# Transformer layer on one core: token parts held against both weight parts in one product of 512 columns, and half of the key transposes moved from TensorE to VectorE and DMAs

## Time and profile before

| what | value |
|---|---|
| median of 3 runs | 1308.89 us (1308.15 to 1309.69) |
| the profiled execution's own time | 1308.92 us |
| its span (first to last instruction) | 1307.1 us |
| granted TensorE clock | 0.999 of 2.4 GHz |
| PE busy | 1287.2 us, 98% |
| DVE busy | 1144.3 us, 88% |
| POOL busy | 830.8 us, 64% |
| ACT busy | 707.8 us, 54% |
| DMA engines busy (mean of 16) | about 24% |

### The profile page before, as it was taken

The page is one execution under the profiler, slowest core; times in us unless marked ns, Lnnn a source line. Parts: engine busy times, 40 slices in busy tenths (PEclk is TensorE's granted clock), DMA queues, the critical chain, the costliest instruction groups (busy, mean ns, idle before and its releaser), DMA issues.

```text
span 1307.1 us, 55818 instructions
## 1 busy us (share of the span) xinstructions
PE 1287.2 (98%) x24160; PEld 1116.5 (85%) x24160; DVE 1144.3 (88%) x2686; ACT 707.8 (54%) x1487; POOL 830.8 (64%) x673
## 2 busy tenths in 40 slices
PE   5999999999999999999999999999999999999998
PEld 4888888888888888888888888888888888888887
DVE  7988898888898888988888988889888889888885
ACT  5645655455654456554555544565545555445552
POOL 2676665765666756657656667566576566675554
PEclk9999999999999999999999999999999999999999
DMA  5012212222222222222222222221222222222211
GB/s 185 14 56 73 78 50 51 80 78 78 65 61 56 79 78 79 51 51 81 78 79 64 67 51 78 78 78 51 51 80 78 79 64 67 51 78 63 61 35 34
DMA packets 175860, 88.54 MB, mean 68 GB/s; under 512 B 135552, under 2 KB 171264, under 8 KB 171520
## 3 DMA queue, kind: packets, MB, share of 16 engines
q1 hardware_dynamic: 174912, 83.97, 22.6%
q10 hardware_dynamic: 704, 1.01, 0.2%
HBM read 53.18 MB, written 17.04 MB: 54 GB/s over the span
## 4 chain that ended last, share of the span: by engine, by line
PE 95%; DVE 3%; POOL 1%; issue 1%; ACT 0%; DMA 0%; DVEq 0%; POOLq 0%
PE ring L343 51%; PE scores L343 17%; PE ring L466 7%; PE ring L482 6%; PE scores L415 5%; PE state_sum L429 4%; PE ring L488 2%; PE scores L397 2%; DVE sm L895 1%; POOL xn L731 0%; DMA x_t<-in_L_attn_x_dram 0%; PE scores L352 0%; POOL rstd L722 0%; DVE stats L819 0%; POOL x_t L748 0%
## 5 line engine op out<-in xcount | busy, mean ns | idle before, releaser
L757 POOL TENSOR_TENSOR hid<-hid,cwb 128x512 f32<-128x512 f32 x128 | 166.4, 1300 | 181.8 <-DVE hid L924 181.0
L916 DVE SCALAR_TENSOR_TENSOR cT<-xT,conv_ws,cT 128x512 f32<-128x512 f32 x192 | 275.1, 1471 | 0.0
L745 POOL TENSOR_TENSOR x_t<-x_t,same 128x1024 f32<-128x1024 f32 x32 | 76.9, 2404 | 254.9 <-ACT same L618 254.9
L639 ACT ACTIVATE sg<-ring 128x512 f32<-128x512 f32 x128 | 76.6, 599 | 268.5 <-PE ring L343 268.5
L343 PE MATMUL ring<-xl,wgu_h 128*128 128x512 f32 x512 | 213.1, 416 | 0.0
L761 POOL TENSOR_TENSOR hl<-hid,hh 128x512 fp32r<-128x512 f32 x128 | 208.8, 1632 | 0.0
L343 PE MATMUL ring<-xh,wgu_l 128*128 128x512 f32 x512 | 201.0, 393 | 0.3 <-issue 0.3
L343 PE MATMUL ring<-xh,wgu_h 128*128 128x512 f32 x512 | 200.5, 392 | 0.0
L569 ACT ACTIVATE yh<-yT 128x256 fp32r<-128x256 f32 x128 | 53.5, 418 | 246.7 <-DVE yT L933 246.7
L902 DVE TENSOR_TENSOR state_bd<-state_sum,tables_s 128x256 f32<-128x256 f32 x248 | 104.0, 419 | 93.8 <-PE state_sum L429 90.6
L895 DVE TENSOR_TENSOR sm<-scores,causal_s 128x512 f32<-128x512 f32 x256 | 157.7, 675 | 6.0 <-PE scores L415 5.0
(11 more groups left out here) (134 smaller groups left out, 3453.4 us busy)
## 6 DMA issues: line engine op xcount, KB each, us to landing
cwb<-cw_rows SPq DMA_DIRECT2D x32, 1024.0 KB, 4.6
x_t<-in_L_attn_x_dram SPq DMA_DIRECT2D x32, 512.0 KB, 4.2
out_dram<-x_t SPq DMA_DIRECT2D x31, 512.0 KB, 2.9
xT<-qks_tok SPq DMA_DIRECT2D x896, 16.0 KB, 1.8
cw_rows<-cwt SPq DMA_DIRECT2D x128, 2.0 KB, 1.4
sm<-in_L_attn_wqkv_dram ACTq DMA_DIRECT2D x2, 384.0 KB, 5.0
sm<-in_L_ffn_Wg_dram SPq DMA_DIRECT2D x2, 256.0 KB, 3.8
sm<-in_L_ffn_Wu_dram SPq DMA_DIRECT2D x2, 256.0 KB, 4.6
```

The costliest lines, as they stand in the source:

```text
L639: act.activation(sg[:, :], GB[t % 2], ACT.Silu).then_inc(s_sg, 1)
L745: pool.tensor_tensor(xb, xb, same[:, :, :], ALU.add).then_inc(s_base1, 1)
L757: pool.tensor_tensor(hid[:, e, :], hid[:, e, :], cwb[:, e, :], ALU.mult).then_inc(s_hid, 1)
L916: ins = dve.scalar_tensor_tensor(out=cT[:, c, :], in0=xT[:, third(s, j, 0), c, LEAD - HALO + n:LEAD - HALO + n + BT], scalar=conv_ws[:, c, ...
```

## The change

- **Output stage.** The weights `wd` and `wo_s` hold low and high part side by side (512 columns). `both_parts` multiplies the high token part by both at once (512 columns, a whole bank), then the low token part by the high weights (256 columns, right half of the bank). The bank holds two sums, and VectorE adds both to x, one after the other.
- **Keys.** For all batches but the first, TensorE transposes the keys of tiles 0 and 1 alone (4 transposes in place of 8). `turn_keys` on VectorE transposes those of tiles 2 and 3 in blocks of 32 x 32 into `kb` (the room of `hid[:, 2]`), and `place_keys` moves the blocks to `ktok` with 16 DMAs of 16 KB from SyncE. VectorE waits for them before it writes `hid[:, 2]`, TensorE before the state sum of tile 2.
- **Taps.** Where the next batch is turned by blocks, ScalarE makes the products of taps 1 to 3 (`tap_terms`, six activations of 128x512 from SBUF into the PSUM banks `SB[0:2]`), and VectorE only adds them (`add_terms`). TensorE waits for the third before it writes the keys' banks.
- **DMAs of the turned input.** 24 of the 32 stay with SyncE, 8 go to ScalarE, one after each of its steps from `silu(1)` to `high_y(2)`.
- **Fill.** 12 waits after each of the first three experts of an output tile (8 in the first batches) and 6 (2) at the batch's start, in place of 38 at its start.
- **Statistics.** Batch 1 takes the statistics of batch 3 after tile 0 and of batch 4 where those of batch 3 stood; before, those of batch 4 came at the batch's very end.

```diff
-    FILL = 38
+    FILL = 12
-        wd_h, wd_l = sb("wd_h", [P, E, D], F32R), sb("wd_l", [P, E, D], F32R)
+        wd = sb("wd", [P, E, 2, D], F32R)
+        wd_l, wd_h = wd[:, :, 0, :], wd[:, :, 1, :]
...
+        kb = hid[:, 2, :].rearrange("p (a t g i) -> p a t g i", a=QUADS, t=2, g=C)
+        TB = SB[0:2]
...
SyncE, spread_cw:
+                if k:
+                    place_keys(s, j, k, range(1))
                 sp.wait_ge(cw_out, at(s, j, 16 * P // BLK, (k + 1) * 16 * P // BLK))
...
+            def place_keys(s, j, k, quarters):
+                sp.wait_ge(s_kturn, at(s, j, 1, k))
+                for a in quarters:
+                    for q in range(QUADS):
+                        sp.dma_start(ktok[a * BLK:(a + 1) * BLK, 2:4, :, q * BLK:(q + 1) * BLK],
+                                     kb[q * BLK:(q + 1) * BLK, a, :, :, :]).then_inc(ktok_in, 16)
SyncE, batch:
-                    place_turned(s, j, 2)
+                    place_turned(s, j, 2, 0, range(QUADS))
+                    place_turned(s, j, 2, 1, range(QUADS // 2))
                 if left:
                     spread_cw(s, j, 1)
+                    place_keys(s, j, 1, range(1, QUADS))
TensorE, heads:
+                if k and by_blocks(s, j, k):
+                    pe.wait_ge(s_conv, at(s, j, HALO, HALO))
...
-                    for t in range(T):
+                    for t in range(T // 2 if k else T):
TensorE, state_sum:
+                if n == T and s + j:
+                    pe.wait_ge(ktok_in, keys_at(s, j, k))
TensorE, batch:
+                def both_parts(dst, hi, lo, w, first=False, final=False):
+                    mm(dst[:, 0:2 * D], hi, w, start=first, stop=False, skip_group_check=True)
+                    return mm(dst[:, D:2 * D], lo, w[:, D:2 * D], start=False, stop=final, skip_group_check=True)
...
+                def fill(n):
+                    for _ in range(n if by_blocks(s, j, 1) else n - 4):
+                        pe.wait_ge(tables_in, 16)
...
                         ins = add_hidden(t, dst, e)
+                        if e < E - 1:
+                            fill(FILL)
...
-                if not last and by_blocks(s, j, 1):
-                    for _ in range(FILL):
-                        pe.wait_ge(tables_in, 16)
+                fill(FILL // 2)
ScalarE:
+            def place_turned(s, j, n):
+                if n == 0:
+                    act.wait_ge(s_turn, at(s, j, 1, 3 - BY_PE))
+                    act.wait_ge(s_halo, at(s, j, 1, 1))
+                a, q = QUADS // 2 + n // QUADS, n % QUADS
+                row = xT[q * BLK:(q + 1) * BLK, third(s, j, 2), 1, LEAD:LEAD + BT]
+                act.dma_start(row.rearrange("p (t a n) -> p t a n", t=T, a=QUADS)[:, :, a, :],
+                              xb_t[a * BLK:(a + 1) * BLK, 1, q, :, :]).then_inc(xT_in[1], 16)
...
+                def tap_terms(n):
+                    if n == 1:
+                        act.wait_ge(s_sm, at(s, j, U * ROWS, U * ROWS))
+                    else:
+                        act.wait_ge(s_conv, at(s, j, HALO, n - 1))
+                    for c in range(C):
+                        first = LEAD - HALO + n
+                        ins = act.activation(TB[c][:, :], xT[:, third(s, j, 0), c, first:first + BT], ACT.Copy,
+                                             scale=conv_ws[:, c, n:n + 1])
+                    ins.then_inc(s_tapped, 1)
order: silu(1) DMA high_hid(0) DMA tap_terms(1) DMA high_y(1) DMA silu(2) DMA high_hid(1) DMA tap_terms(2) DMA
       high_y(2) DMA silu(3) high_hid(2) tap_terms(3) high_y(3) high_hid(3)
VectorE:
+            def turn_keys(s, j, k):
+                for g in range(C):
+                    dve.wait_ge(s_kT, at(s, j, C, k * C + g + 1))
+                dve.wait_ge(s_hl, at(s, j, T, 3))
+                for t in range(2):
+                    ins = dve.transpose(kb[:, :, t, :, :].rearrange("p a g i -> p g a i"),
+                                        kT[:, :, (2 + t) * P:(3 + t) * P].rearrange("p g (a n) -> p g a n", n=BLK))
+                ins.then_inc(s_kturn, 1)
...
+                    for c in range(C):
+                        ins = dve.tensor_tensor(cT[:, c, :], TB[c][:, :], cT[:, c, :], ALU.add)
+                    ins.then_inc(s_conv, 1)
...
                     router(s, j, 1)
+                    turn_keys(s, j, 1)
                     key_sums(s, j, 1)
...
-                    dve.tensor_tensor(xb, done[:, 0:D], xb, ALU.add).then_inc(s_out, 1)
+                    own(dve.tensor_tensor(xb, done[:, 0:D], xb, ALU.add))
+                    dve.tensor_tensor(xb, done[:, D:2 * D], xb, ALU.add).then_inc(s_out, 1)
```

More of the change, by code:

```diff
@@ L300, in spread_cw, with place_turned @@
                              cw_rows.rearrange("r n -> (r n)").partition_broadcast(P)).then_inc(cw_in, 16)
-            def place_turned(s, j, k):
+            def place_turned(s, j, k, c, quarters):
                 sp.wait_ge(s_turn, at(s, j, 1, k + 1 - BY_PE))
                 sp.wait_ge(s_halo, at(s, j, 1, k - 1))
[L307 to L312, removed]
+                for a in quarters:
+                    for q in range(QUADS):
+                        row = xT[q * BLK:(q + 1) * BLK, third(s, j, k), c, LEAD:LEAD + BT]
+                        sp.dma_start(row.rearrange("p (t a n) -> p t a n", t=T, a=QUADS)[:, :, a, :],
+                                     xb_t[a * BLK:(a + 1) * BLK, c, q, :, :]).then_inc(xT_in[c], 16)
+            def place_keys(s, j, k, quarters):
+                sp.wait_ge(s_kturn, at(s, j, 1, k))
+                for a in quarters:
+                    for q in range(QUADS):
+                        sp.dma_start(ktok[a * BLK:(a + 1) * BLK, 2:4, :, q * BLK:(q + 1) * BLK],
+                                     kb[q * BLK:(q + 1) * BLK, a, :, :, :]).then_inc(ktok_in, 16)
             def batch(s, j, left):
@@ L493, in add_attention @@
                     pe.wait_ge(s_yl, at(s, j, T, t + 1))
[L494 to L495 removed]
+                    for c in range(C):
+                        both_parts(dst, yh[:, c, ts], yl[:, c, ts], wo_s[:, c, :, :].rearrange("p a n -> p (a n)"))
                 def add_hidden(t, dst, e, first=False):
                     ts = slice(t * P, (t + 1) * P)
[L499 to L500 removed]
+                    return both_parts(dst, hh[:, e, ts], hl[:, e, ts], wd[:, e, :, :].rearrange("p a n -> p (a n)"),
+                                      first=first, final=e == E - 1)
+                def fill(n):
+                    for _ in range(n if by_blocks(s, j, 1) else n - 4):
+                        pe.wait_ge(tables_in, 16)
                 def output(t):
@@ L669, in batch @@
                 high_y(0)
+                placing = left > 1 and by_blocks(s, j, 2)
                 silu(1)
+                if placing:
+                    place_turned(s, j, 0)
                 high_hid(0)
+                if placing:
+                    place_turned(s, j, 1)
+                if ahead:
+                    tap_terms(1)
+                if placing:
+                    place_turned(s, j, 2)
                 high_y(1)
+                if placing:
+                    place_turned(s, j, 3)
                 if not last and not ahead:
@@ L679, in batch @@
                 high_hid(1)
+                if placing:
+                    place_turned(s, j, 5)
+                if ahead:
+                    tap_terms(2)
+                if placing:
+                    place_turned(s, j, 6)
                 high_y(2)
+                if placing:
+                    place_turned(s, j, 7)
                 silu(3)
                 high_hid(2)
+                if ahead:
+                    tap_terms(3)
                 high_y(3)
@@ L774, in batch @@
                         low_x(s, j, 1, c)
+                if by_blocks(s, j, 3) and not by_blocks(s, j, 2):
+                    normalise(s, j, 2)
                 weigh(1)
@@ L789, in batch @@
                     base(s, j, 1)
-                if left > 1 and not by_blocks(s, j, 2):
+                if left > 1 and not by_blocks(s, j, 3):
                     normalise(s, j, 2)
@@ L908, in batch, with add_terms @@
                 last = left == 0
+                def add_terms(n):
+                    if n == 1:
+                        dve.wait_ge(s_tap0, at(s, j, 1, 1))
+                    else:
+                        dve.wait_ge(s_conv, at(s, j, HALO, n - 1))
+                    dve.wait_ge(s_tapped, (s * BPS + j - BY_PE + 1) * HALO + n)
+                    for c in range(C):
+                        ins = dve.tensor_tensor(cT[:, c, :], TB[c][:, :], cT[:, c, :], ALU.add)
+                    ins.then_inc(s_conv, 1)
                 def tap(n):
+                    if not last and by_blocks(s, j, 1):
+                        add_terms(n)
+                        return
                     if n == 1:
@@ L923, in gate_up @@
                     dve.wait_ge(s_up, at(s, j, T, t + 1))
+                    if t == 2 and s + j:
```

(10 more changed lines are left out.)

16 lines of the change are left out of this document (13 added, 3 removed).

## The result

In 20 runs of each kernel the time went from 1308.97 us (1308.15 to 1309.69) to 1311.32 us (1310.68 to 1312.26): ratio 1.0018, 95% interval 1.0012 to 1.0024. That is no gain but a loss of 2.35 us: the interval excludes 1, and its size is at the edge of the 0.2% that the prediction said can be told from no change. The forecast was 1294.5 us. The profiled execution has a span of 1309.0 us (1307.1 before) at the same granted clock, 0.999.

A forecast was written before the change was run, and what follows sets the result against it. PE was taken as the bound, its start-to-start distances making about 39.9 us a batch. 28 batches x (0.435 + 0.19 - 0.10) = 14.7, less 0.2, gave 14.5 us off 1308.92: 1294.5 us, range 1288 to 1308.

The forecast's parts named there:

- that of ScalarE: ScalarE's queue: six more activations and 8 DMA issues of 0.60 us fit into its gaps and cost nothing.
- Together about 0: First batches: 0.9 us new wait against 0.62 gained, three times, perhaps 0.5 for statistics, against a 1.2 us stall removed.
- output tiles: PE's output stage: 12 products instead of 18 save 0.05 us a tile, 0.19 us a batch; bounds 0 and 0.27.
- fill: Waits spread through PE's output stage: charged 0.1 us a batch, bounds 0 and 0.3.
- key transposes: PE's key stage: four of eight transposes go at 0.109 us each, saving 0.435 us a batch in 31 batches.
- VectorE's output chain: VectorE from router to last addition: starts 0.7 us earlier, grows by 0.72 and 1.78, just fits with 0.1 to 0.2 spare.
- last batch, in all: Program's end: the last batch adds one addition (0.44 us) and saves 0.2 us on PE.
- VectorE's chain: Rival at the batch's start: VectorE's longer output chain makes PE's numerators wait; 1299 to 1306 us, chance 0.15.
- The fill does not pace PE: Denies the rival that output-stage waits cost 0.3 us a batch instead of 0.1: 1300, up to 1304 us, chance 0.12.
- The slow rival: ScalarE's DMAs wait for SyncE's, up to 1.29 us per issue; silu late, PE stands about 0.85 us a batch; 1317, chance 0.12.
- It decides from about 1.05 us per issue: Threshold for ScalarE's and SyncE's queues blocking each other: below 1.05 us per DMA issue, silu(3) is on time.
- It does little: Rival on PE: columns stay the same and small stalls eat the transposes' 0.435 us; 1306 to 1311 us, chance 0.06.

The follow-up runs named there:

- Experiments 5: Kernel before with one change: 8 of the 32 DMAs of the turned input moved from SyncE to ScalarE; 1320.49 us, ratio 1.0086.
- experiment 6: Kernel after with the two ScalarE DMAs that fell into PE's bursts moved behind `high_y(2)` and `silu(3)`; 1304.0 us, ratio 0.9962 to the kernel before.
- 9: Kernel before with 8 DMAs on ScalarE and SyncE's 24 held until VectorE has written y of tile 2; run once, 1315.26 us beside 1309.08.
- experiment 7: Kernel after with batch 1's statistics in the order of the kernel before; 1309.8 us, ratio 1.0003 to the kernel before.
- 4: Kernel after with all eight key transposes on PE, no key DMAs, and 8 fill waits left out; 1320.17 us, ratio 1.0084 to the kernel before.
- 8: Kernel before with only the output stage changed: 512-column products, two additions, spread fill of 11 and 12; 1306.6 us, ratio 0.9981.
- experiment 3: Kernel after without any of the fill; 1333.45 us, ratio 1.0181 to the kernel before.
- experiments 1: Kernel after with all 32 DMAs of the turned input on SyncE again; 1366.3 us, ratio 1.0433 to the kernel before.
- experiments 2: Kernel after with all taps on VectorE again, the DMAs left on ScalarE; 1329.81 us, ratio 1.0156 to the kernel before.

## Why the prediction was wrong

**The step that failed** is that of ScalarE: six activations and 8 DMA issues, "Cost nothing". ScalarE's own queue is indeed on time, and its issues take about 0.60 us as taken (median 0.593). The step looked only for who waits for ScalarE and at the time the issue takes. It didn't ask what else runs while two queues issue. The runs show 0.19 + 0.27 = 0.46 us a batch on PE, 28 x 0.46 = 12.9 us in all. Experiments 5, 6 and 9 tie it to both queues being at it beside a burst of short products.

**"Together about 0"** for batches 0 to 2 was the second: +5.5 us, 3.1 of it by the statistics in batch 1 (experiment 7). I had counted these at half a microsecond. The rest of the chain, with taps still on VectorE there, I had at 0.9 us three times; PE waited 1.05, 1.56 and 1.07 us for the last addition at the start of batches 1, 2 and 3, which is 1.0 us more in sum.

**Where the 16.4 us between forecast and spans went** (14.5 forecast as gain, 1.9 measured as loss). In the 27 steady batches 0.52 - 0.16 = 0.36 is missing in each, 9.8 us: 0.46 for ScalarE's DMAs and 0.05 for the output tiles, less 0.10 for the fill, which cost nothing, and about 0.04 in stages that moved by less than 0.02 each. The first four batches make 6.0 (5.5, and 0.5 that was forecast as the gain of batch 3), the two ends of the program 0.5.

**Terms against forecast**, us a batch:

| term | forecast | measured | by |
|---|---|---|---|
| key transposes | -0.435 | -0.44 | stages, 4 |
| output tiles | -0.19 | -0.14 | stages, 8 |
| fill | +0.10 | 0 | 3 |
| VectorE's output chain | 0 | 0 | stages |
| ScalarE's DMAs | 0 | +0.46 | 5, 9 |
| first batches, in all | 0 | +5.5 | stages, 7 |
| last batch, in all | +0.24 | +0.64, and +0.13 ahead of batch 0 | stages, spans |

The output term was mis-sized in its pitch: it used that of products among their like, 0.228 and 0.118 us; in the mixed tile the experts' 512-column products lie 0.232 us before the next, and a tile saves 0.035 us, not 0.05. The Trainium skill (TensorE: Matmul & The Clock Gate, "Back-to-back issue gap") gives the 2.5 ns for an isolated warm product; the 0.06 us a batch worked out from it is an estimate, and the 0.14 measured decides.

**The rivals.** VectorE's chain did not become the bound: additions 0.42 to 0.45 us apart, as taken. The fill does not pace PE. The slow rival named the right two queues and the wrong mechanism: all 224 issues of ScalarE overlap one of SyncE, and yet 194 took 0.59 to 0.65 us, 29 up to 0.85 and one 1.65. So the lock that the Trainium skill describes (Perfetto Trace Analysis, "DMA Instruction — HWDGE (DVE, Sync)") is not visible in these durations. "It decides from about 1.05 us per issue" asked for a late silu, and the loss came without one. "It does little" comes closest to the measured time, with 1306 to 1311, and that is luck: no small stalls ate the transposes' 0.435 us, they were gained in full and given back in the bursts.

What stays open: why two queues slow the burst. The first half of a burst runs at its old pace: up to the 57th product the starts lie as before, to 1 ns in the mean of 18 bursts of tile 1 in the kernel after. The lag grows from about the 65th to 0.20 us at the 97th, and the last 16 add nothing. In experiment 6, where ScalarE's issue is over by then, the lag (0.08 us) falls into the same part. Nothing waits on a semaphore, so it looks like PE's supply of instructions; no run shows this.

## What to carry to other kernels

When instructions move to an engine that has time, check also what their neighbours in time are: a DMA issue that nobody waits for can still cost where a second queue issues beside a burst of small products. Move one part alone first; the kernel before with only the moved DMAs showed at once what the whole change hid. And a change of a steady state wants its own sum for the batches in which the steady conditions don't hold yet.

## What the hardware showed

- Bursts of 112 products of 32 to 64 columns take 1.75 us with one queue issuing 16 KB block moves beside them, whichever it is (the kernel before and experiments 1 and 9), and 1.92 to 2.08 in the mean with SyncE and ScalarE both issuing (the kernel after, experiments 2 to 5 and 7). Most issues themselves stay at about 0.60 us. Long products (128x512) next to the same DMAs keep their pace (gate/up 1 is 2.97 us before and 2.96 after).
- Waits that are always fulfilled are free between products of the output stage (experiment 3: the same to 0.01 us), and taking them all away cost 22 us, most of it in a stage elsewhere (scores after tile 0, 1.85 instead of 1.14 us).
- In this kernel's order of work a SyncE queue of 48 such moves a batch of 39.8 us is too full (gate/up 0 4.30 us), 44 nearly so (3.09), and 40 fit (2.87).
